# Weight turns moved, two layer norms shared out, and a wider pitch of the lag weights in HBM

## The reference

```
r = layernorm(x);  k = v = ctx
# per sequence, scanned along its 128 tokens in both directions
A_t = sum over i != t of exp((|t-i|-1) w + k_i) v_i      # per channel
B_t = the same without v_i
x  += tanh(g_xattn) * sigmoid(r) * (A_t + e^(u+k_t) v_t) / (B_t + e^(u+k_t))
z   = layernorm(x)
xq  = fake_quant(z) with one scale for the tensor (max |z|, clip factor)
h   = fake_quant(silu(xq Wg^T) * (xq Wu^T)),  again one scale
x  += tanh(g_ffn) * h Wd^T          # weights fake-quantised per row; I = 704
```

## Time and profile before

| | |
|---|---|
| median of 3 runs (lowest to highest) | 252.05 us (251.74 to 253.44) |
| the profiled execution: its time / its span | 254.3 us / 252.6 us |
| granted TensorE clock, mean | 0.853 |
| busy: TensorE / VectorE / ScalarE / GpSimd | 171.3 / 163.7 / 154.6 / 99.4 us |
| head: first instruction to TensorE's first chunk | 0 to 41.5 us |
| lag stage: to the end of the last residual | 41.5 to 129.0 us |
| norm stage: to FFN's first product | 129.0 to 159.3 us |
| read / written in HBM | 27.53 / 4.46 MB |

### The profile page before, as it was taken

How to read it: one execution, slowest core, us unless ns; L and a number is a source line. 1 busy time by engine, 2 the same in 40 slices (tenths; PEclk the granted TensorE clock), 3 DMA queues, 4 the chain that set the end, 5 groups by cost and what they waited for, 6 DMA issues and landing times.

```text
span 252.6 us, 3143 instructions
## 1 busy us (share of the span) xinstructions
PE 171.3 (68%) x1030; PEld 122.0 (48%) x1034; DVE 163.7 (65%) x343; ACT 154.6 (61%) x198; POOL 99.4 (39%) x117
## 2 busy tenths in 40 slices
PE   0008876999194795799705475799595994589970
PEld 0003334999193795799704354243232341366640
DVE  0894373255225046088877865359979799899993
ACT  4599962133617246254329996699777794589700
POOL 2586000044022043044367540047354476007992
PEclk9999998999779589799956655599989799689995
DMA  4999979999899069196000000000000000002358
GB/s 125 347 345 349 284 214 247 266 267 288 198 304 263 2 184 282 35 242 176 1 0 3 0 0 0 0 1 4 0 0 0 0 0 0 0 0 86 125 187 271
DMA packets 49279, 32.16 MB, mean 127 GB/s; under 512 B 2289, under 2 KB 49009, under 8 KB 49265
## 3 DMA queue, kind: packets, MB, share of 16 engines
q1 hardware_dynamic: 49120, 31.73, 43.7%
q10 hardware_dynamic: 144, 0.26, 0.3%
HBM read 27.53 MB, written 4.46 MB: 127 GB/s over the span
## 4 chain that ended last, share of the span: by engine, by line
PE 46%; ACT 29%; DVE 13%; POOL 4%; issue 3%; DMA 2%; DVEq 1%; SPq 0%; POOLq 0%
PE ps L798 23%; PE ps L872 10%; ACT z_t L399 8%; PE ps L906 7%; ACT hidden L418 5%; ACT z_t L425 3%; ACT w_int L433 2%; POOL hidden L360 2%; PE ps L785 2%; DVE h_peaks L714 2%; DVE h_space L748 2%; DMA x_all<-in_x 2%; ACT w_intb L441 2%; DVE hidden L703 2%; PE ps L821 2%
## 5 line engine op out<-in xcount | busy, mean ns | idle before, releaser
L798 PE MATMUL ps<-hidden 128*128 128x128 f32 (+1 forms) x512 | 64.9, 295 | 2.5 <-DVE hidden L551 2.5
L798 PEld LDWEIGHTS ps<-hidden 128*128 128x128 f32 x512 | 64.6, 211 | 3.3 <-issue 3.3
L343 POOL TENSOR_TENSOR x_all<-x_all,silu_out 128x512 f32<-128x512 f32 x16 | 24.4, 1526 | 80.8 <-DVE silu_out L613 80.8
L604 DVE SCALAR_TENSOR_TENSOR h_space<-z_t,ps 128x256 f32<-128x256 f32 x32 | 13.4, 418 | 46.1 <-PE ps L798 46.0
L407 ACT ACTIVATE up_out<-h_space 128x512 f32<-128x512 f32 x16 | 10.1, 630 | 47.9 <-DVE h_space L604 47.9
L785 PE MATMUL ps<-hidden,flip 128*128 128x512 f32 x32 | 17.0, 686 | 22.1 <-DMA hidden<-in_ctx 19.7
L872 PE MATMUL ps<-xq,wuT 128*128 128x512 bf16 (+1 forms) x96 | 26.0, 416 | 6.3 <-DVE hidden L703 6.3
L872 PE MATMUL ps<-xq,wgT 128*128 128x512 bf16 (+1 forms) x92 | 25.7, 420 | 3.5 <-ACT xq L501 3.2
L906 PE MATMUL ps<-wdT,z_t 128*128 128x256 bf16 (+1 forms) x192 | 25.4, 288 | 2.6 <-ACT z_t L535 2.6
L714 DVE TENSOR_REDUCE h_peaks<-hidden (+2 forms) x24 | 26.1, 1121 | 0.4
L821 PE MATMUL ps<-ident,hidden 128*128 128x128 f32 x64 | 14.5, 400 | 16.7 <-ACT hidden L418 16.7
(11 more groups left out here) (82 smaller groups left out, 258.7 us busy)
## 6 DMA issues: line engine op xcount, KB each, us to landing
hidden<-lag_w SPq DMA_DIRECT2D x32, 512.0 KB, 5.2
x_all<-in_x SPq DMA_DIRECT2D x8, 512.0 KB, 8.1
hidden<-in_ctx SPq DMA_DIRECT2D x8, 512.0 KB, 9.2
out<-x_all SPq DMA_DIRECT2D x16, 256.0 KB, 2.1
xq<-in_L_ffn_w_down SPq DMA_DIRECT2D x1, 704.0 KB, 4.2
xq<-in_L_ffn_w_gate SPq DMA_DIRECT2D x1, 640.0 KB, 6.4
h_space<-in_L_ffn_w_up SPq DMA_DIRECT2D x1, 640.0 KB, 5.8
lag_w<-silu_out ACTq DMA_DIRECT2D x1, 255.0 KB, 7.2
```

What stands on the lines that cost most here:

```text
L343: nc.gpsimd.tensor_tensor(xs, xs, mixed[:, m % 2, :, :].rearrange("p c b -> p b c"), ALU.add).then_inc(s["x1_done"], 1)
L798: last = nc.tensor.matmul(ps[:, j % BANKS, c * 2 * SEQS:end * 2 * SEQS], lag_tile(j)[:, c, :], ekp[:, (j * CK + c) * 2 * SEQS:(j * CK + en ...
```

## The change

- `lag_dram` has the shape [128, 2, 1088]: a channel's 255 lag weights stand 1088 floats (4352 bytes) behind the former channel's, 255 before. The store writes 256 rows of 1020 bytes, the loads step by 1088.
- Groups 0, 2, 4 and 6 of the first norm are normalised by VectorE (`normalise1`, four tensor_scalar of 256 elements, into the new tile `z1`, two buffers), and ScalarE takes one exp over the group's 1024 elements. `normalise1(g)` stands behind `stats1(g+1)` in VectorE's queue. `lag_w` moves to `up_out` to free the space.
- The fourth sequence of each group of the second norm is normalised by GpSimd (`normalise_last`); `rstd2(g+1)` stands ahead of `normalise_last(g)`. TensorE and VectorE wait for both shares. `peak_z` runs three groups behind the statistics, two before.
- Weight steps: turns behind chunks 14, 21 and 27 (10, 14, 20); the scales of matrices 1 and 2 behind pairs 6 and 9 (5, 8); storing 0, 1, 2 at reciprocals 8, 11, 14 (6, 8, 11); quantising 1 and 2 at 8 and 11 (6, 9). The Sync queue's order and quantisation 0 are as before.

```diff
@@ -59,6 +59,7 @@
     PAIRS = CHUNKS // 2
     CG = C // P
     LAGS = 2 * T - 1
+    PITCH = 1088
     SLOTS = 6
     BANKS = 6
     HALF = CK * SEQS
@@ -115,7 +116,10 @@
         rden = late[:, 0:2 * 512].rearrange("p (s n) -> p s n", s=2)
         mixed = late[:, 2 * 512:4 * 512].rearrange("p (s c b) -> p s c b", s=2, b=SEQS)
         lnd = up_out[:, 0:512]
-        lag_w = late[:, 0:CG * LAGS].rearrange("p (i j) -> p i j", i=CG)
+
+        DVE_Z = 0, 2, 4, 6
+        z1 = late[:, 0:2 * GC].rearrange("p (s n) -> p s n", s=2)
+        lag_w = up_out[:, 512:512 + CG * LAGS].rearrange("p (i j) -> p i j", i=CG)
         lag_row = down_row[:, :, :].rearrange("p j c -> p (j c)")[:, 0:LAGS]
 
         xq_flat = xq[:, :, :, :, :].rearrange("p a b c d -> p (a b c d)").bitcast(F32)
@@ -128,7 +132,7 @@
         silu_even = [silu_out[:, 0, :], h8_space[:, 0:BT]]
         up_even = [up_out[:, :], h8_space[:, BT:2 * BT]]
 
-        lag_dram = nc.dram_tensor("lag_w", [P, CG * LAGS], F32, kind="Internal")
+        lag_dram = nc.dram_tensor("lag_w", [P, CG, PITCH], F32, kind="Internal")
 
         ps = stack.enter_context(nc.psum_tensor("ps", [P, 8, 512], F32))
         TURN = 6
@@ -193,8 +197,8 @@
 
             "ctx_back", "ek_done", "pk_done", "ab_done", "den_done", "ln_done", "rden_done", "mix_done", "x1_done",
 
-            "bn1_done", "mv1_done", "ve1_done", "rs1_done", "sc1_done", "ez_done",
-            "bn2_done", "mv2_done", "ve2_done", "rs2_done", "sc2_done", "z_done", "zT", "z_kept", "peak_done",
+            "bn1_done", "mv1_done", "ve1_done", "rs1_done", "sc1_done", "z1_done", "ez_done",
+            "bn2_done", "mv2_done", "ve2_done", "rs2_done", "sc2_done", "z_done", "z_last", "zT", "z_kept", "peak_done",
 
             "top_done", "topT",
 
@@ -244,7 +248,7 @@
                     sp.wait_ge(s["ctx_back"], before + 1)
                 else:
                     sp.wait_ge(s["ab_done"], before - GROUPS + 1)
-                src = bass.AP(lag_dram, j * CK * LAGS, [[1, P], [LAGS, CK], [1, T]])
+                src = bass.AP(lag_dram, j * CK * PITCH, [[1, P], [PITCH, CK], [1, T]])
                 sp.dma_start(lag_tile(j), src).then_inc(ring_in[(GROUPS + j) % SLOTS], 16)
 
             def load_weights(m):
@@ -347,8 +351,18 @@
                 rstd1(g)
             for m in range(PAIRS):
                 residual(m)
+            def normalise_last(g):
+
+                n = g * GS + GS - 1
+                pool.wait_ge(s["sc2_done"], g + 1)
+                nc.gpsimd.tensor_scalar(z_all[:, n * C:(n + 1) * C], x_all[:, n * C:(n + 1) * C], rs2[:, n:n + 1],
+                                        mr2[:, n:n + 1], ALU.mult, ALU.add).then_inc(s["z_last"], 1)
+
+            rstd2(0)
             for g in range(GROUPS):
-                rstd2(g)
+                if g + 1 < GROUPS:
+                    rstd2(g + 1)
+                normalise_last(g)
 
 
             with pool.Fori(0, BLOCKS // 2) as pair:
@@ -384,7 +398,7 @@
                 act.wait_ge(s["lag_done"], CG)
                 nc.scalar.activation(lag_w[:, :, T - 1], wu[:, CG:2 * CG], ACT.Exp).then_inc(s["lag_done"], 1)
                 act.wait_ge(s["lag_done"], CG + 1)
-                act.dma_start(lag_dram[:, :], lag_w.rearrange("p i j -> p (i j)")).then_inc(s["lag_stored"], 16)
+                act.dma_start(lag_dram[:, :, 0:LAGS], lag_w).then_inc(s["lag_stored"], 16)
 
             def exp_k(g):
                 act.wait_ge(s["ctx_back"], g + 1)
@@ -392,6 +406,12 @@
 
             def exp_z(g):
 
+                if g in DVE_Z:
+                    act.wait_ge(s["z1_done"], DVE_Z.index(g) + 1)
+                    nc.scalar.activation(ez[:, :, g * GS:(g + 1) * GS],
+                                         z1[:, DVE_Z.index(g) % 2, :].rearrange("p (b c) -> p c b", c=C),
+                                         ACT.Exp).then_inc(s["ez_done"], 1)
+                    return
                 act.wait_ge(s["sc1_done"], g + 1)
                 xs = seqs(x_all[:, :], g * GS, GS)
                 for i in range(GS):
@@ -413,7 +433,7 @@
 
                 act.wait_ge(s["sc2_done"], g + 1)
                 xs = seqs(x_all[:, :], g * GS, GS)
-                for i in range(GS):
+                for i in range(GS - 1):
                     n = g * GS + i
                     last = nc.scalar.activation(z_all[:, n * C:(n + 1) * C], xs[:, i, :], ACT.Identity,
                                                 scale=rs2[:, n:n + 1], bias=mr2[:, n:n + 1])
@@ -475,16 +495,15 @@
                 if m == 4:
                     quantise_weights(0)
                     cast_weights(0)
-                if m == 6:
+                if m == 8:
                     keep_weights(0)
                     quantise_weights(1)
                     cast_weights(1)
-                if m == 8:
+                if m == 11:
                     keep_weights(1)
-                if m == 9:
                     quantise_weights(2)
                     cast_weights(2)
-                if m == 11:
+                if m == 14:
                     keep_weights(2)
                 if m == 12:
                     exp_clips()
@@ -573,6 +592,17 @@
                     last = nc.vector.bn_aggr(mv1[:, g * GS + i, :], bn1[:, i, :])
                 last.then_inc(s["mv1_done"], 1)
 
+            def normalise1(g):
+
+                i = DVE_Z.index(g)
+                dve.wait_ge(s["sc1_done"], g + 1)
+                wait(dve, s["ez_done"], DVE_Z[i - 2] + 1 if i >= 2 else 0)
+                for k in range(GS):
+                    n = g * GS + k
+                    last = nc.vector.tensor_scalar(z1[:, i % 2, k * C:(k + 1) * C], x_all[:, n * C:(n + 1) * C],
+                                                   nr1[:, n:n + 1], mr1[:, n:n + 1], ALU.mult, ALU.add)
+                last.then_inc(s["z1_done"], 1)
+
             def stats2(n, h):
                 return nc.vector.bn_stats(bn2[:, n, h, :], x_all[:, n * C + h * P:n * C + (h + 1) * P])
 
@@ -616,6 +646,7 @@
 
             def peak_z(g):
                 dve.wait_ge(s["z_done"], g + 1)
+                dve.wait_ge(s["z_last"], g + 1)
                 nc.vector.tensor_reduce(peaks[:, g:g + 1], z_all[:, g * GC:(g + 1) * GC], AX.X, ALU.max,
                                         apply_absolute_value=True).then_inc(s["peak_done"], 1)
 
@@ -634,6 +665,8 @@
 
             for g in range(GROUPS):
                 stats1(g)
+                if g - 1 in DVE_Z:
+                    normalise1(g - 1)
             for g in range(GROUPS):
                 product(g)
             dve.wait_ge(s["tanh_done"], 1)
@@ -649,11 +682,10 @@
                 mix(2 * m + 1)
                 if m == 3:
                     weight_scales(0)
-                if m == 5:
+                if m == 6:
                     weight_scales(1)
-                if m == 8:
+                if m == 9:
                     weight_scales(2)
-                if m == 9:
                     dve.wait_ge(s["ident_set"], 2)
                     down_diagonals()
                 if m == 13:
@@ -663,13 +695,12 @@
                     early_stats(done, n)
                     done += n
             assert done == SEQS
-            late_stats(0)
-            late_stats(1)
-            for g in range(2, GROUPS):
+            for g in range(GROUPS):
+                if g >= 3:
+                    peak_z(g - 3)
                 late_stats(g)
-                peak_z(g - 2)
-            peak_z(GROUPS - 2)
-            peak_z(GROUPS - 1)
+            for g in range(GROUPS - 3, GROUPS):
+                peak_z(g)
 
             def global_peak(tile, prefix, quotient, scale, inverse):
 
@@ -812,6 +843,7 @@
 
             def turn_z(g):
                 pe.wait_ge(s["z_done"], g + 1)
+                pe.wait_ge(s["z_last"], g + 1)
                 if g == 1:
                     pe.wait_ge(s["w_stored"], 3)
                 wait(pe, s["z_kept"], g - 2)
@@ -827,12 +859,8 @@
                 reverse(g)
             for j in range(CHUNKS):
                 accumulate(j)
-                if j == 10:
-                    turn_weights(0)
-                if j == 14:
-                    turn_weights(1)
-                if j == 20:
-                    turn_weights(2)
+                if j in (14, 21, 27):
+                    turn_weights((14, 21, 27).index(j))
             for g in range(GROUPS):
                 turn_z(g)
```

## The result

The kernel after takes **235.49 us** (median of 4 runs, 232.62 to 235.92) against 252.75 us of before beside it; the ratio is 0.929, with a 95% interval of 0.922 to 0.936, so some 17 to 18 us less. The forecast was 236.5 us with a range of 230 to 243.5. Two further executions of it took 233.74 and 235.20 us. Medians take in every execution timed beside before, the ratios the faster ones alone, so the two can differ by a few us. The profiled execution took 232.62 us with a span of 230.5 us, 2.9 us under the median, while that of before lay above its own, so the two profiles lie further apart (22.1 us of span) than the medians do.

What follows compares the result with a forecast made beforehand. Bound: TensorE waiting for ScalarE's weight casts in the lag stage, ScalarE in the second norm's stage. Terms −12.5 (turns), 0 (pitch), −0.6 and −2.5 (norms) sum to −15.6 us: 252.05 to 236.5 us, range 230 to 243.5.

Steps and rivals of the forecast that it cites:

- The turns: Lag stage: three gaps where TensorE waits for weight casts, 21.5 us, go; 9.0 us come back; net −12.5 us.
- the first wait that was put back: Lag stage, chunk 15: waits 3.2 us for its lag load behind w_down's; with 1.55 us of slower clock, 4.75 us.
- turn 2: Lag stage, after chunk 27: waits 2.1 us for its cast; with a fallen clock 4.3 us given back.
- level with TensorE: Lag loads from 70 to 76 us: 1.79 us per 512 KB, TensorE's pace, so no further load waits.
- The pitch: Lag rows 1088 floats apart in HBM, their store and loads: counted as 0 us.
- The first norm: Head: VectorE normalises four of eight groups, ScalarE takes one 1024-element exponential each: −0.6 us, bounds −1.9 and +2.1.
- The second norm: Norm stage: GpSimd takes one normalisation per group, period from 2.88 to about 2.45 us: −2.5 us, bounds −3 and +0.5.
- Rival (a): Lag stage: both given-back waits stay small; 232.8 us for the clocks alone, 227.5 with nothing given back; chance 0.20.
- Rival (c): Both norms: VectorE held up behind GpSimd at their exclusive port, GpSimd's operation 1.1 us; +2.7 and +3.0, 242 us; chance 0.12.
- (b): Lag stage: the wait moves to ScalarE and VectorE, turn 1 misses its cast too; 7.5 us worse, 244; chance 0.13.
- (d): Lag stage: spread rows slow the lag loads; gain gone at 2.8 us per load, 257 us at 3.0; chance 0.04.
- (e): Lag stage: the stall only moves from one weight to the next, 252 us; chance 0.02.

Runs made afterwards that it cites:

- experiment 8: The kernel after with the load of w_down behind lag load 17 in the Sync queue instead of behind 14: 230.98 us, ratio 0.919.
- experiment 1: The kernel before with the weight steps (turns) moved alone: 232.32 us, ratio 0.928.
- experiment 7: The kernel after with VectorE writing its normalised first-norm group channel by channel, so ScalarE reads neighbouring floats: 232.97 us, ratio 0.916.
- experiment 2: The kernel before with the pitch of 1088 floats alone: 251.89 us, ratio 1.000.
- experiment 3: The kernel before with the first norm shared with VectorE alone: 252.83 us, ratio 1.004.
- experiment 4: The kernel before with the second norm shared with GpSimd and the peaks reordered alone: 249.99 us, ratio 0.996.
- experiment 9: The kernel after with VectorE's group written channel by channel, w_down's load behind lag load 17 and three small loads behind lag load 25: 230.44 us, ratio 0.913.
- experiment 11: The kernel after with the lag rows packed again, 255 floats apart: median 235.55 us, executions from 229.90 to 270.79 us.
- experiment 12: The kernel after with VectorE's group written channel by channel, w_down's load behind lag load 17, small loads ahead of all lag loads: 230.02 us, ratio 0.910.
- experiment 5: The kernel after once more, no edit: 233.95 us, ratio 0.932.
- experiment 6: The kernel after with no group of the first norm given to VectorE: 232.74 us, ratio 0.929.
- experiment 10: The kernel after with w_down's load behind lag load 17, small loads behind lag load 25, no first-norm share for VectorE: 230.52 us, ratio 0.912.

## Why the prediction was right

**The turns.** Forecast: 21.5 us of gaps go, 9.0 come back, net 12.5. Measured alone: 18 to 19.5 us. All three gaps went, and the first wait that was put back is there at its place, for its reason, and nearly at its size (2.95 for 3.2 us; experiment 8 shows the reason).

What was mis-sized is what comes back: 4.5 us of waits in the kernel after (2.95, 1.20 and 0.34), and in experiment 1 4.7 us (2.72 and 0.43 of waits, 1.6 of clock), for 9.0. The clock didn't fall behind the first wait in the kernel after, so 1.55 us were not paid there; in experiment 1 they were. And turn 2 did not wait 2.1 us and then turn at half clock, in any profile with the turns moved: 0.43 us was its longest wait. I had carried over the 1.77 us of the diagonals, which in the earlier trace rows ran beside GpSimd's residual; in their new place they run alone in 0.59. ScalarE was also ahead of my reckoning, cast 2 being over at 97.75 instead of 102.2. The waits of 1.2 and 0.3 us for loads 21 and 28 I had excluded: "level with TensorE" left no room for the Sync queue's small loads, which stand in the chain ahead of load 21; ahead of load 28 it shows the transfer alone.

A further 1.6 us of the stage's gain is no doing of the turns. The first chunks of before ran at half clock, those of the kernel after and of experiment 1 did not, while the forecast left them as they were. With it the stage adds up: 21.5 less 4.5 plus 1.6 is 18.6 us, and it measured 18.4. The last chunk ended at 107.0 us, 5 us sooner than the forecast had it.

**The pitch.** Forecast 0, measured 0.1 us (interval ±0.5%), with landings 1.7 to 1.8 us apart in both layouts. By the rule of the Trainium skill (DMA: Bandwidth & Descriptors, section "How a descriptor splits into AXI transactions") there was to be no gain either; that the reason is the one it names, no run shows.

**The first norm.** Forecast −0.6 us, measured +0.8 us of head, +1.1 us of time. This step failed in its sign. The failed part was the price "I price at the 1.02 us of L391, 1024 elements in the same order": L391 reads PSUM, and in SBUF the same order costs 1.97 us (experiment 7 gives 1.06 with neighbouring reads). VectorE's four operations took 1.36 to 1.38 us for the 1.1 that I had taken; the groups' shares ended at 26.5 us, where 26.4 was forecast, but exponential 6 ran 1.96 us from 26.88, behind exponential 5 and the first exp(k). With neighbouring reads the head is 0.3 us shorter than without the share (41.04 against 41.32 us): the sign of the forecast and half of its size.

**The second norm.** Forecast −2.5 us; the stage gave 2.2 to 2.6 us, GpSimd's operation 0.555 us for the 0.55 taken, the period 2.5 for 2.45. Of the whole time only 1.0 us by the ratio (interval −2.1 to +0.1) could be seen.

**The sum** came out near, 15.6 forecast and 17.3 by the medians, and that nearness is in good part luck: the gain of the turns was set too low by some 6 us, and those of the first norm (by 1.3 to 1.7 us) and of the second (by up to 1.5 us) too high. These errors do not balance. Made alone, the parts sum to 20.1 us by their medians, 2.8 us more than the whole change brought, and the turns alone measured as much as the whole change; where the rest went is open, the stages ahead of FFN having kept it. Rival (a), waits that stay small, was the truer account of the lag stage. Its ground, that TensorE kept full speed behind pauses near 1 us, holds for the stretch from 30 to 38 us of before (clock 1.00), but not for its norm stage, where behind pauses of 0.9 us the clock was 0.50 from 145 to 157 us. Rival (c) was half true, a slower head by another mechanism: VectorE's groups, each with GpSimd's `rstd1` beside it, were not held up by the 0.8 us that the port was to cost. Of (b), (d) and (e) nothing was seen.

## What to carry to other kernels

A step that waits in an in-order queue costs more than its idle time: here 4.5 to 5.3 us of idleness cost 6 to 8 us each, the rest being the clock behind it, and moving the step until its input was there gave all of it back but for the next waits in line. Look for that next wait before moving, in the DMA queue too: the load that waits for a semaphore, and the small loads whose issue takes 2.7 us in a full queue. Take the price of an operation from a row with the same memory and the same steps, not from one with the same element count.

## What the runs showed of the hardware

ScalarE's read of 1024 floats from SBUF in steps of 1024 bytes took 1.97 us against 1.06 us for neighbouring ones, while the same steps in PSUM took 1.02. VectorE's two diagonals took 0.59 us alone and 1.77 to 1.79 us in before and experiments 2 to 4, each time beside a residual of GpSimd of 1.53 or 1.54 us. The same pause of 2.46 us ahead of the first chunk was followed by some 3 us at a clock of 0.50 in six of the profiled executions (before and experiments 2, 4, 9, 11 and 12; in 2 and 12 after some 1 us at full speed) and by full clock in the eight others (after and experiments 1, 3, 5, 6, 7, 8 and 10); it costs 1.6 us. Behind the wait ahead of chunk 15 it was the same: 2.72 us were followed by half clock in experiment 1, and 2.38 to 2.97 us by full clock in the kernel after and in experiments 5, 6, 7 and 11. The length of the pause does not decide it alone. And a wider pitch of rows in HBM, 4352 bytes for 1020, changed nothing that was measured of loads of 512-byte pieces.
